# First three tiles of expert 0 as a unit of their own, filled from the first six batches and zero rows

## The reference

```python
x = x + tanh(g_xattn[0]) * xattn(layernorm(x), ctx, ctx)   # sigmoid(Q^T K / 16), then V
# experts, on xf = layernorm(x) with M = 2048 rows of H = 512
t = xf * rsqrt(mean(xf * xf) + EPS) * norm_w
logits = t @ gate_w.T + gate_b
vals, idx = top_k(logits, 4);  gates_k = softmax(vals)
h = einsum('mh,eoh->emo', t, w1) + b1                       # 512 -> 1024
a = minimum(h[..., ::2], 7);  b = clip(h[..., 1::2], -7, 7)
act = a * sigmoid(1.702 * a) * (b + 1)
y = einsum('emi,edi->emd', act, w2) + b2                    # 512 -> 512
x = x + tanh(g_ffn[0]) * einsum('me,emd->md', G, y)
```

## Time and profile before

| | us |
|---|---|
| median of 3 runs | 849.22 (846.76 to 851.21) |
| the profiled execution | 851.6 |
| its span | 849.8 |
| PE busy | 780.2, 92% of the span |
| DVE / ACT / POOL busy | 504.1 / 445.9 / 311.3 |

### The profile page before, as it was taken

How to read it: one execution, slowest core, us unless ns; L and a number is a source line. 1 busy time by engine, 2 the same in 40 slices (tenths; PEclk the granted TensorE clock), 3 DMA queues, 4 the chain that set the end, 5 groups by cost and what they waited for, 6 DMA issues and landing times.

```text
span 849.8 us, 16473 instructions
## 1 busy us (share of the span) xinstructions
PE 780.2 (92%) x3972; PEld 651.1 (77%) x3973; DVE 504.1 (59%) x1006; ACT 445.9 (52%) x771; POOL 311.3 (37%) x290
## 2 busy tenths in 40 slices
PE   5999998248999999999999999999999999999984
PEld 2544554237888899988889888899998988898873
DVE  2677666415676665566576664756557575746540
ACT  3445533115566575556557655646556565646540
POOL 0157575730433325233324323334333333325212
PEclk9999999559999999999999999999999999999997
DMA  8565654051586576348558654556535554544212
GB/s 288 177 198 176 230 163 111 20 139 51 125 229 145 125 214 165 58 138 208 123 163 212 173 114 131 148 136 148 148 57 151 107 150 131 156 123 74 37 25 38
DMA packets 107766, 116.98 MB, mean 138 GB/s; under 512 B 11808, under 2 KB 77344, under 8 KB 107744
## 3 DMA queue, kind: packets, MB, share of 16 engines
q1 hardware_dynamic: 88896, 77.32, 29.3%
q0 software_dynamic: 18848, 39.40, 23.6%
HBM read 88.06 MB, written 28.94 MB: 138 GB/s over the span
## 4 chain that ended last, share of the span: by engine, by line
PE 80%; DVE 7%; issue 7%; ACT 3%; DMA 1%; POOL 0%; DVEq 0%; ACTq 0%; POOLq 0%; SPq 0%; another core or an unknown queue 0%
PE ps L525 37%; PE ps L474 25%; PE ps L378 7%; PE ps L389 6%; PE ps L453 3%; DVE W1l L1028 1%; DVE uu L1017 1%; PE ps L406 1%; DVE hv L1019 1%; DVE bv L1015 1%; ACT hTh L698 1%; ACT bw L678 1%; PE ps L397 1%; ACT sg L675 1%; DVE ps L988 1%
## 5 line engine op out<-in xcount | busy, mean ns | idle before, releaser
L525 PE MATMUL ps<-xTh,W1h 128*128 x768 | 260.7, 339 | 10.2 <-issue 6.9
L525 PE MATMUL ps<-xTh,W1l 128*128 x768 | 255.0, 332 | 0.0
L525 PE MATMUL ps<-xTl,W1h 128*128 x768 | 255.0, 332 | 0.0
L1175 POOL DMA_INDIRECT out<-ys,dgI x75 | 118.8, 1584 | 309.2 <-ACT ys L657 285.2
L525 PEld LDWEIGHTS ps<-xTh,W1h 128*128 128x128 f32 x768 | 145.9, 190 | 20.4 <-issue 15.3
L525 PEld LDWEIGHTS ps<-xTh,W1l 128*128 128x128 f32 x768 | 145.8, 190 | 5.4
L525 PEld LDWEIGHTS ps<-xTl,W1h 128*128 128x128 f32 x768 | 146.0, 190 | 5.1
L474 PE MATMUL ps<-W2h,hTh 128*128 x300 | 120.3, 401 | 5.6 <-DVE hTl L1023 5.6
L474 PE MATMUL ps<-W2l,hTh 128*128 x300 | 118.1, 394 | 0.0
L474 PE MATMUL ps<-W2h,hTl 128*128 x300 | 117.9, 393 | 0.0
L657 ACT ACTIVATE ys<-ps,dgI 128x512 f32<-128x512 f32 x75 | 51.7, 689 | 124.2 <-DVE ps L988 120.2
(11 more groups left out here) (130 smaller groups left out, 995.4 us busy)
## 6 DMA issues: line engine op xcount, KB each, us to landing
W1f<-in_wts SPq DMA_DIRECT2D x64, 512.0 KB
W2f<-in_wts SPq DMA_DIRECT2D x32, 512.0 KB
X<-in_x SPq DMA_DIRECT2D x8, 512.0 KB, 6.3
Kt<-in_ctx SPq DMA_DIRECT2D x8, 512.0 KB
Vt<-in_ctxT SPq DMA_DIRECT2D x8, 512.0 KB
rows<-tt SPq DMA_DIRECT2D x8, 512.0 KB
out<-base SPq DMA_DIRECT2D x8, 512.0 KB
b2s<-in_bias SPq DMA_DIRECT2D x16, 256.0 KB
```

Source lines behind the costliest of these rows:

```text
L525: m = e.matmul(P_[i % 2][:, 0:64 * w], (W1h, W1l)[wl][:, i, 2 * k + h, :], (xTh, xTl)[xl][:, bass.ds(par, 1), k, 0:64 * w], start=(t == 0) ...
L1175: e.indirect_dma_start(out, bass.IndirectOffsetOnAxis(dgI[:, j, 0:1].bitcast(I32), axis=0), ys[j][:], None, compute_op=ALU.add).then_inc(d ...
```

## The change

Expert 0's first `SOON` = 3 tiles become unit 0, of 384 columns, whose rows come from the first `BSOON` = 6 batches. `fill_up` on DVE counts what is lacking to 384 (here 97) and adds that many to the running counts before batch 6 is ranked, so that these places keep their zero row. SP reads the three columns of row numbers into `soon` once the 48 writes of six batches have landed, POOL gathers the three tiles before it writes the places of the last two batches, and the engines compute unit 0 in straight code ahead of the loop. What is left of expert 0 (435 + 97 - 384 = 148 rows) becomes unit 1, with two tiles and 256 columns. There are now 25 units and 76 tiles. The first layers of expert 0 cover 384 + 256 = 640 columns instead of 448. In the first turn that adds to `out`, POOL waits between the three adds of unit 0, since several tiles hold the same zero rows.

```diff
+SOON = 3
+BSOON = 6
+NTILES = M * K // 128 + E - 1 + SOON
+        P0 = (ps[4], ps[5], ps[1])
+        P1 = (ps[4], ps[1], ps[3], ps[0])
...
             store_rows(B - 1)
+            e.wait_ge(d_put, 16 * 2 * K * BSOON)
+            e.dma_start(soon[:], places[:, 0, 0:SOON, :]).then_inc(d_soon, 16)
+            store_base(B - 1)

             e.wait_ge(d_put, 16 * 2 * K * B)
...
-            store_base(B - 1)
-
-            e.wait_ge(d_base, 16 * B)
...
+            turn_soon(0)
             rank(B - 1)
             e.wait_ge(v_mm, 2 * B)
             e.matmul(RK[:, 64:64 + E], ones[:], MM[:, B, 0, :], start=True, stop=True).then_inc(t_cnt, 1)
+            for j in range(1, SOON):
+                turn_soon(j)
+            e.wait_ge(e_lop, 3)
+            e.wait_ge(e_lo1, N1)
+            e.wait_ge(e_xl, SOON + 1)
...
+            soon_pair(0)
+            soon_pair(1)
             e.wait_ge(v_q, 7)
...
+            soon_pair(2)
+            soon_pair(3)
...
+            e.wait_ge(e_lo2, N2)
+            e.wait_ge(e_hl, 8)
+            for j in range(SOON):
+                outputs(j, 0)
...
+            for j in range(4):
+                turned_in(now, j, P1[j])
+            with e.Fori(1, n) as u:
...
+            for j in range(SOON):
+                high_x(j, j + 1, 0, P0[j])
+            e.wait_ge(e_b1, 2)
+            e.copy(bcur[:], b1s[:, 0, :, :]).then_inc(e_bc, 1)
+            e.wait_ge(e_bc, 1)
+            for i in range(4):
+                gate(0, i, 128 * SOON)
+                if i:
+                    kept(0, i - 1, 128 * SOON)
+            kept(0, 3, 128 * SOON)
...
+            def fill_up():
+                e.wait_ge(t_c0, 1)
+                e.tensor_scalar(lack[:, 0:1], RK[:, 96:97], -1.0, C[:, C_LACK:C_LACK + 1], op0=ALU.mult, op1=ALU.add).then_inc(v_lack, 1)
+                had = MM[:, BSOON, 0, 0:1]
+                for k in range(SOON):
+                    e.wait_ge(v_lack, k + 1)
+                    to = had if k == SOON - 1 else lack[:, k + 1:k + 2]
+                    e.scalar_tensor_tensor(to, lack[:, 0:1], 128.0 * k, had if k == 0 else lack[:, k:k + 1], ALU.is_gt, ALU.add).then_inc(v_lack, 1)
...
             choose(B - 1)
+            low_x(0, 1, 0, P0[0])
             places(B - 1)
             gates(B - 1)
+            for j in range(1, SOON):
+                low_x(j, j + 1, 0, P0[j])
...
+            for i in range(4):
+                hidden(0, i, 128 * SOON)
+                low_h(0, i, 128 * SOON)
+                if i == 0:
+                    e.wait_ge(t_te, 1)
+                    e.tensor_tensor(te[:].rearrange("p t r -> p r t"), LG[:, 64:64 + 6 * NUP].rearrange("p (r t) -> p r t", r=6),
+                                    C[:, C_BASE:C_LATE].rearrange("p (r t) -> p r t", r=6), ALU.add).then_inc(v_te, 1)
...
             x1_scale(B - 1)
+            e.wait_ge(d_soon, 16)
+            e.wait_ge(d_zrow, 16)
+            for i in range(2):
+                e.wait_ge(d_rows[i], 16 * (B // 2))
+            for j in range(SOON):
+                e.indirect_dma_start(xg[j][:], None, rows, bass.IndirectOffsetOnAxis(soon[:, j, 0:1].bitcast(I32), axis=0)).then_inc(d_g[j], 16)
             put(B - 2)
             put(B - 1)
...
+                        if u is not None and 0 < j < SOON:
+                            with e.If(u < 2):
+                                e.wait_ge(d_s, 16 * j)
```

More of the change, by code:

```diff
@@ L134, in build @@
         idx = sb("idx", [128, (E + 1) * TE + 3, 2])
+        soon = sb("soon", [128, SOON, 2])
+        lack = sb("lack", [128, 3])
         tt = [sb(f"tt{i}", [128, 2, H]) for i in range(2)]
@@ L470, in second_layer @@
                             e.wait_ge(e_ys, free)
[L471 to L477, removed]
+                        outputs(j, bass.ds(slot, 1))
             e.wait_ge(v_te, 3)
@@ L483, in pe @@
             turned, done = e.alloc_register("pe_turned"), e.alloc_register("pe_done")
[L484 to L489, removed]
+            for j, r in enumerate(landed):
+                e.reg_mov(r, 16 if j < SOON else 0)
+            e.reg_mov(turned, SOON)
+            e.reg_mov(done, SOON)
+            load_fields(e, now, 1, 0)
+            load_fields(e, nxt, 2, 0)
             e.reg_mov(was[F_NT], 0)
@@ L500, in pe @@
                 wide = e.snap(now[F_HL], min_val=1, max_val=8)
[L501 to L510, removed]
+                ready = e.snap(e.snap(turned, min_val=SOON, max_val=NTILES + 24) + 1)
                 for i in range(4):
@@ L518, in pe @@
                     e.sem_inc(e_gp, 1)
[L520 to L528, removed]
                     def pick(ws):
                         if len(ws) == 1:
-                            part(ws[0])
+                            pair(u, i, bass.ds(par, 1), ws[0])
                         else:
@@ L689, in second @@
                             gated(j)
-                def turned_in(i):
-                    with e.If(more > LESS[i]):
-                        e.reg_add(turned, turned, 1)
-                        high_x(i, e.snap(turned, min_val=5, max_val=NTILES + 24), bass.ds(odd, 1))
-                def kept(i, w):
-                    e.wait_ge(e_h, e.snap(u * 4 + (i + 1)))
-                    e.copy(hTh[:, i, 0:w], hv[i % 2][:, 0:w]).then_inc(e_hh, 1)
                 def next_high(i):
@@ L886, in dve @@
                     places(b - 2)
+                if b == BSOON + 1:
+                    fill_up()
                 if b == 0:
@@ L1028, in low_w @@
                         e.tensor_tensor(W1l[:, i, :, :], W1f[:, i, :, :], W1h[:, i, :, :].bitcast(F32), ALU.subtract).then_inc(e_lo1, 1)
-                def turned_in(i):
-                    with e.If(more > LESS[i]):
-                        e.reg_add(split, split, 1)
-                        low_x(i, e.snap(split, min_val=5, max_val=NTILES + 24), bass.ds(odd, 1))
                 def by_width(f):
@@ L1152, in gathers @@
                         gather(j)
-            e.wait_ge(e_tx, 4)
-            place(row(nxt), 2)
+            e.wait_ge(d_idx0, 16)
+            e.wait_ge(e_tx, SOON)
+            place(row(nxt), 1)
             gathers(nxt)
+            e.wait_ge(d_idx, 16)
             e.wait_ge(d_zero, 16)
@@ L1178, in pool @@
                 take(e.snap(u + 1))
-                add_back()
-                e.wait_ge(e_tx, e.snap(given, min_val=4, max_val=NTILES + 24))
+                add_back(u)
+                e.wait_ge(e_tx, e.snap(given, min_val=SOON, max_val=NTILES + 24))
                 e.sem_inc(e_go, 1)
-                place(row(fut), e.snap(u + 3))
+                place(row(fut), e.snap(u + 2))
                 gathers(fut)
```

216 lines of the change are left out of this document (127 added, 89 removed).

## The result

The changed kernel takes 868.76 us (median of 4 runs, 867.47 to 871.72), the kernel before on the same chip 849.96 (846.76 to 851.21): a ratio of 1.0232, 95% interval 1.0191 to 1.0273. Slower by 2.3%, and outside the range. The profiled execution has a span of 868.1 us, 18.3 more than before's.

The account below looks back on a forecast made before the run. PE was taken as the bound, apart from a nearly idle hole of some 30 us. X of 226.6 against 225.2 loses 1.4 us: 853.0 on the profiled 851.6, less 2.4 for the median, 850.6; range 844.8 to 856.2.

Parts of the forecast that it names:

- tail: After unit 0's last pair, ACT and DVE element work with nothing left to hide it: 4.75 us, ending at 185.0.
- second layer of unit 0: 36 matmuls on PE behind the tail's gap, partly at the low clock: 11.2 us, ending at 196.1.
- unit 1 to the end of its last pair: Unit 1's four pairs of 256 columns on PE, from 199.9, with pair 0 at 4.0 us: ending near 218.
- pair 0 of unit 2: PE's first pair of unit 2, just before the mark: 5 us, 24 matmuls of 0.21.
- PE at the mark: PE's own work reaches the turn of unit 3's tile 0 at 223, or 228 if the clock stays low.
- X: Time of PE's turn of unit 3's tile 0: 226.6, set by the gather behind unit 0's three adds, 5.5 us landing each.
- Unit 0 on PE: 96 first-layer matmuls of 384 columns, 14 at low clock: 19.0 us, plus 0.3 for the unit list, done at 180.2.
- Rival (d): PE's clock stays low through unit 1, in bursts between waits: mark at 228 to 229, 852 to 854 us; chance 0.12.
- Early gather: Read of `soon` behind the last store takes 2.6 us, a gather 3.82; third gather lands at 157.1, unit 0 starts at 160.9.
- Counting: `fill_up`, four small DVE instructions before batch 7: some 1 us, hidden in a 4.06 us DVE wait.
- rival (a): Unit 0's adds land later, each us counting twice: loss passes 4.25 us from 6.9 us landing, 854.6 at 7.5; chance 0.17.
- The mark and the balance: At PE's turn of unit 3's tile 0, gain only if X is below 225.2; each us of X is one us of time.

Follow-up runs that it names:

- for two tiles: The changed kernel with `SOON` = 2 in place of 3, so unit 0 has 256 rows and no zero rows: 859.85 us, ratio 1.0079 to the kernel before.
- the 8 writes beside the pairs above: Changed kernel with two tiles, own zero rows, no waits between unit 0's adds, batch 6's eight writes ahead of unit 0's gathers: ratio 1.0108, pairs 15.7 us.

## Why the prediction was wrong

| step | forecast | measured |
|---|---|---|
| unit 0 starts | 160.9 | 163.2 |
| four pairs and the list | 19.3 | 27.3 |
| tail | 4.75 | 4.3 |
| second layer of unit 0 | 11.1 | 11.2 |
| turns to unit 1 | 3.8 | 3.2 |
| unit 1 to the end of its last pair | 18.1 | 19.7 |
| pair 0 of unit 2 | 5 | 9.4 |
| PE at the mark | 223 | 238.3 |
| gather behind the adds, X | 226.6 | 240.3 |

- **The step that failed is "Unit 0 on PE"**, "19.0 us, and 0.3 for the unit list between: done at 180.2". Its matmuls were priced rightly and then laid beside 16 table writes as if these touched POOL alone; the writes were costed only for the table they delay. They held up PE, DVE and ScalarE for 8.0 of the 15.3 us by which PE came late to the mark. Taking them away, or only putting GpSimd's computing there, gives the forecast's figure back (19.7, 20.1); reads in their place don't (28.1). No rival had this, and the forecast excluded, from unit 0's inputs alone, that it is not computed beside the writes. One small sign stood in the trace of before, where the list's second matmul came 2.1 us behind the first, though its inputs were there at 162.6 (PE's timeline); a second trace of that code has 0.15 us there:

```profile
164.74 0.27 PE L447 MATMUL ps<-Q,ones 16*128 16x108 bf16 x1 [1.77 <-remote]
```

- **The next is pair 0 of unit 2**, 4.4 us over its 5: the gap of 2.9 and then the low clock, which rose only 2.8 us into the pair. Rival (d) came nearest: PE's work in pieces with waits between. The Trainium skill ("TensorE: Matmul & The Clock Gate", HAM oscillation) says that such bursts start cold; the granted clock of 0.77 behind the gap agrees. What the gap itself waited for is, by the times of the loads above, most likely the loop's code. With the stall gone this stretch still keeps X at 233.85, so that the forecast would have been wrong by some 7 us without the stall too.
- **Early gather:** the table read took 2.59 as against 2.6, the gather 4.39 as against 3.8. Unit 0 began 2.3 us late, 0.6 by the gather and 1.7 by the last batch. That batch came later than before's; the shift was not tried by itself, and earlier batches differ by as much both ways.
- **Counting, tail, second layer, restart:** right within 0.6 us each. The second layer by stretch has a clock of 0.74, as in the earlier trace rows:

```profile
194.70:206.10 11.40, 11.19 (x36) 8.68 (x36) 0.74 0.00 1
```

- **Unit 1** took 1.6 us more; ScalarE was 2.2 us late in it, without a wait in the program that explains it.
- **The adds** landed in 5.08 and 7.16 us, not 5.5 each, and their starts lay 6.2 and 8.2 apart. So rival (a) was half right. But the forecast made them the bound over PE, and here they were 2.0 us behind PE's 238.3. With their waits gone the time hardly moves. The 2.6 us that the forecast estimated from the Trainium skill ("DMA: Bandwidth & Descriptors", Anatomy of one DMA) are half of the shorter landing here.
- **The mark and the balance** held to some 3 us: 15.1 us lost at the mark, 18.3 in the span; for two tiles 228.21 - 225.2 = 3.0 at the mark and 4.2 in the span (854.0 against 849.8) of the profiled run, the fastest of eight, whose median lost 6.4.

## What to carry to other kernels

A hole in PE is not free for use because the DMA engines and PE are idle in it: look at what GpSimd issues there, and price new code beside a long run of its indirect transfers (16 here; 8 did far less) by the end of these transfers, not by its own instructions. A first unit cut off from the loop brings a tail, a restart and a narrow unit behind it, and these are paid even where the stall isn't; here the narrow unit was over before the loop's code was loaded. And where two chains end within 2 us of each other, removing the wait that ends last shows almost nothing.

## What the runs showed of the hardware

While GpSimd issued 16 or more indirect transfers in a row, 1.27 us each and 8 bytes a partition in all but the two or three gathers among them, with the DMA engines 2 to 12% busy, the other engines' instructions came late, by up to 4.6 us on DVE and 10 us on ScalarE, on PE down to one matmul in 2.1 us (the run with reads), and all recovered within 4 us of the last one.

Neither the code nor the transfers do it alone. The same code without the transfers doesn't stall (19.7 us). And behind 262 us, where the loop repeats, 133 indirect transfers are issued and the longest idle time under issue or remote is this, in ScalarE's timeline:

```profile
281.41 0.69 ACT L724 ACTIVATE ys<-ps,dgI 128x512 f32<-128x512 f32 x1 [2.03 <-issue]
```

That the code must run for the first time does not follow from this, since the loop's transfers come at most four in a row. It is not enough either: the first stage's loop over batches is a loop of the Python program, so that its code is straight and runs once as well, and 48 table writes run beside it, eight in a row; yet PE has no idle time over 0.6 us under issue or remote between 30 and 150 us, in the change and in the kernel before. So the length of the run of transfers seems to count, as with the 8 writes beside the pairs above. No run has 16 in a row beside code that repeats.

PE's late matmuls wait for no signal, which points to the loading of instructions. The Trainium skill ("Runtime: NRT & Kernel Launch", Instruction fetch mechanics) says that each engine's sequencer loads its code in blocks over a DMA queue of its own, and that the cost is mostly hidden. The page of the change lists 23 such transfers over the whole span. Their times agree with a cost that shows in the third unit's gap, but not in the stall: one of 16 KB ends at 160.6, the next starts at 189.4, and none runs between, nor in the stall of any other run with 16 in a row. So what holds the engines up there stays open.
